# Moving the caps of the activations from GpSimd to VectorE in the feed-forward pipeline of a convolution and attention block

## The reference, cut to what matters

```python
def _quantize_activations_groupwise(x):
    n = x.shape[0]
    gs = n // NUM_GROUPS
    xq = jnp.zeros_like(x)
    for g in range(NUM_GROUPS):
        ag = x[g * gs:(g + 1) * gs]
        gamma = jnp.max(jnp.abs(ag))
        xq = xq.at[g * gs:(g + 1) * gs].set(jnp.clip(ag * QB / (gamma + EPS), -QB + EPS, QB - EPS))
    return xq

def _bitlinear(x, W, b):
    Wb = _binarize_weights_groupwise(W)
    y = jnp.einsum('btc,oc->bto', x, Wb) + b
    return _quantize_activations_groupwise(y)

h = _bitlinear(x, W1, b1)                 # 96 -> 384 channels
h = jax.nn.gelu(h, approximate=False)
out = _bitlinear(h, W2, b2)               # 384 -> 96 channels
```

## Time and profile before

| | us |
|---|---|
| median of three runs | 3130.85 (3129.27 to 3132.96) |
| the profiled execution | 3126.59 |
| its span in the trace | 3124.9 |
| TensorE busy | 2841.3 (91%) |
| VectorE busy | 2173.1 (70%) |
| ScalarE busy | 2052.4 (66%) |
| GpSimd busy | 1393.8 (45%) |

### The profile page before, as it was taken

One profiled execution on the slowest core, in us unless ns is written; L12 is line 12 of the kernel. 1 busy time (PEld: TensorE's weight loads), 2 busy tenths in 40 slices (PEclk: granted clock), 3 DMA queues, 4 the chain that ended last, 5 costly groups with the idle time before them and its releaser, 6 DMA issues. The chain is left out here.

```text
span 3124.9 us, 85427 instructions
## 1 busy us (share of the span) xinstructions
PE 2841.3 (91%) x28774; PEld 1733.4 (55%) x28966; DVE 2173.1 (70%) x4403; ACT 2052.4 (66%) x3943; POOL 1393.8 (45%) x2063
## 2 busy tenths in 40 slices
PE   3899999999998589999999999999999979999883
PEld 2445455454544256666666666666666645555541
DVE  3565665656566378888898898889888935455542
ACT  2677777777776357777777777777777745666561
POOL 0143444444343444434444444443444413577778
PEclk9999999999999789999999999999999989999996
DMA  1113232322222367655556565565655523234434
GB/s 32 41 51 107 71 106 70 106 80 96 97 93 82 112 125 117 120 111 119 115 115 119 112 119 116 115 120 111 119 115 115 117 67 96 81 98 125 126 98 107
DMA packets 919803, 315.97 MB, mean 101 GB/s; under 512 B 848257, under 2 KB 904354, under 8 KB 919714
## 3 DMA queue, kind: packets, MB, share of 16 engines
q1 hardware_dynamic: 916258, 313.98, 42.4%
q10 hardware_dynamic: 3456, 0.79, 0.1%
HBM read 113.35 MB, written 99.88 MB: 68 GB/s over the span
## 5 line engine op out<-in xcount | busy, mean ns | idle before, releaser
L939 DVE TENSOR_REDUCE at_unit_max<-at_ps_queries 128x1 f32<-128x512 f32 (+3 forms) x2304 | 1121.1, 548 | 119.7 <-PE at_ps_queries L831 97.5
L905 ACT ACTIVATE at_probs<-at_ps_keys 128x512 f32<-128x512 f32 x1344 | 738.5, 596 | 244.7 <-PE at_ps_keys L845 216.7
L831 PE MATMUL at_ps_queries<-at_turned 96*128 96x512 bf16 (+3 forms) x2304 | 688.0, 330 | 64.3 <-DMA at_turned<-at_spread 31.8
L845 PE MATMUL at_ps_keys<-at_turned 128*128 128x128 bf16 (+3 forms) x3264 | 593.8, 268 | 2.9 <-ACT at_probs L905 2.4
L845 PEld LDWEIGHTS at_ps_keys<-at_turned 128*128 128x128 bf16 x3456 | 255.4, 97 | 241.1 <-ACT at_probs L905 122.6
L865 PE MATMUL at_ps_values<-at_probs,at_v 128*32 128x128 f32 x10752 | 373.4, 276 | 0.5 <-ACT at_probs L905 0.5
L799 POOL TENSOR_TENSOR at_tick<-at_one 128x1 f32<-128x1 f32 x192 | 37.1, 193 | 705.5 <-ACT at_diag_probs L905 460.2
L834 PE MATMUL at_ps_queries<-mask_queries,ident_bf 128*128 128x128 bf16 x1536 | 338.8, 221 | 0.0
L865 PEld LDWEIGHTS at_ps_values<-at_probs,at_v 128*32 128x32 f32 x10752 | 270.6, 109 | 42.3 <-ACT at_probs L905 1.3
L1189 POOL TENSOR_SCALAR ff_hidden<-ff_hidden 128x1024 f32<-128x1024 f32 x90 | 246.9, 2769 | 63.6 <-ACT ff_hidden L1147 63.6
L831 PEld LDWEIGHTS at_ps_queries<-at_turned 96*128 96x128 bf16 x2304 | 217.5, 98 | 100.7 <-DMA at_turned<-at_spread 32.9
(11 more groups left out here) (199 smaller groups left out, 4896.4 us busy)
## 6 DMA issues: line engine op xcount, KB each, us to landing
qkv_rows<-cb_packed SPq DMA_DIRECT2D x32, 1536.0 KB, 8.3
at_stacks<-qkv_rows SPq DMA_DIRECT2D x192, 256.0 KB, 3.2
cb_x<-in_x_dram SPq DMA_DIRECT2D x32, 384.0 KB, 3.7
cb_x_again<-in_x_dram SPq DMA_DIRECT2D x32, 384.0 KB, 4.5
x_after_conv<-cb_x SPq DMA_DIRECT2D x32, 384.0 KB, 5.0
attention_rows<-at_att SPq DMA_DIRECT2D x384, 32.0 KB, 2.1
ff_att_rows<-attention_rows SPq DMA_DIRECT2D x32, 384.0 KB, 3.7
ff_x<-x_after_conv SPq DMA_DIRECT2D x32, 384.0 KB, 4.7
```

What stands on the lines that cost most here:

```text
L831: mm = pe.matmul(pq[:, u % QBANKS, 0:n], QT[0:STACK, slot, qb * P:(qb + 1) * P], KT[0:STACK, slot, k0:k0 + n], start=True, stop=True)
L845: mm = pe.matmul(pk[:, bank_k, c0:c0 + n * P], KT[:, slot, kb * P:(kb + 1) * P], QT[:, slot, q0 * P:(q0 + n) * P], start=(c0 == 0), stop=True,
L905: act.activation(probs, pk[:, (slot * NU + k) % KBANKS, :], ACT.Exp, scale=scale).then_inc(S["probs"], 1)
L939: dve.tensor_reduce(MX[:, r % 2, qb, k0 // BANK:k0 // BANK + 1], pq[:, u % QBANKS, 0:n], AX.X, ALU.max).then_inc(S["unit_max"], 1)
```

## The change

The caps of the activations (`limit`) move from GpSimd's program to VectorE's. For a group's first image caps 0 and 1 stand behind X2 and cap 2 behind the last maximum of the round; for the other images all three stand near the start of the round, ahead of the maximum over Y2. In VectorE's round the first maximum, `peak1(r, 0)`, moves ahead of the wait for GpSimd's power, and the second, `peak1(r, 1)`, moves from before X2 to behind it. GpSimd keeps the power and the output cap (`cap`), and computes that of the next output o + 1 after the power; that of a group's first output stands ahead of the power. In the last group VectorE computes the output caps of images 24 to 27 itself (with a semaphore of their own, `limited_late`), GpSimd those of 28 and 29. SyncE's, TensorE's and ScalarE's programs are unchanged.

```diff
--- before.py
+++ after.py
@@ -1002,7 +1002,7 @@
         b2_loaded = sem("b2_loaded")
         names = ("ones_set half_set att_turned att_copied y_done x2_ready xc_done squares var_sums scale xn_ready "
                  "xn_turned xnt_ready y1_psum y1_copied y1_max max1 all_max1 scale1 gelu h_ready y2_psum y2_ready "
-                 "y2_max max2 all_max2 scale2 limited out_ready").split()
+                 "y2_max max2 all_max2 scale2 limited limited_late out_ready").split()
         S = {n: sem(n) for n in names}
 
         def quarters(dram):
@@ -1184,29 +1184,26 @@
 
             @block.gpsimd
             def _(pool):
-                def limit(s, k):
-                    pool.wait_ge(S["gelu"], 3 * s + k + 1)
-                    pool.tensor_scalar(Y1[:, s % SLOTS, k, :], Y1[:, s % SLOTS, k, :], LIMIT, None, ALU.min
-                                       ).then_inc(S["h_ready"], 1)
+                def cap(o):
+                    pool.wait_ge(S["scale2"], 2 * (o // GB) + 2)
+                    pool.tensor_scalar(Y2[:, o % SLOTS, :, :], Y2[:, o % SLOTS, :, :], M2[:, o // GB, 3:4], LIMIT,
+                                       ALU.mult, ALU.min).then_inc(S["limited"], 1)
+
                 pool.memset(MINUS_HALF[:, :], -0.5).then_inc(S["half_set"], 1)
                 pool.memset(SQ[:, :, C:C + 1], 1e-5).then_inc(S["half_set"], 1)
                 pool.wait_ge(S["half_set"], 2)
                 for r in range(-1, FULL + OUT_LAG):
-                    m, s, o = r + 1, r - LAG, r - OUT_LAG
+                    m, o = r + 1, r - OUT_LAG
+                    if 0 <= o < FULL - GB and o % GB == 0:
+                        cap(o)
                     if 0 <= m < FULL:
                         pool.wait_ge(S["var_sums"], m + 1)
                         _above(pool.wait_ge, S["xn_ready"], m)
                         pool.tensor_tensor(SCALE[:, :], VS[:, :], MINUS_HALF[:, :], ALU.pow).then_inc(S["scale"], 1)
-                    if o >= 0:
-                        pool.wait_ge(S["scale2"], 2 * (o // GB) + 2)
-                        pool.tensor_scalar(Y2[:, o % SLOTS, :, :], Y2[:, o % SLOTS, :, :], M2[:, o // GB, 3:4], LIMIT,
-                                           ALU.mult, ALU.min).then_inc(S["limited"], 1)
-                    if 0 <= s < FULL and s % GB == 0:
-                        for k in range(CHUNKS):
-                            limit(s, k)
-                    if 0 <= s + 1 < FULL and (s + 1) % GB:
-                        for k in range(CHUNKS):
-                            limit(s + 1, k)
+                    if 0 <= o + 1 < FULL - GB and (o + 1) % GB:
+                        cap(o + 1)
+                for o in (FULL - 2, FULL - 1):
+                    cap(o)
 
             @block.vector
             def _(dve):
@@ -1229,6 +1226,11 @@
                                       ).then_inc(S[scale_name], 1)
                     dve.wait_ge(S[scale_name], 2 * g + 1)
                     dve.reciprocal(M[:, g, 3:4], M[:, g, 2:3]).then_inc(S[scale_name], 1)
+
+                def limit(s, k):
+                    dve.wait_ge(S["gelu"], 3 * s + k + 1)
+                    dve.tensor_scalar(Y1[:, s % SLOTS, k, :], Y1[:, s % SLOTS, k, :], LIMIT, None, ALU.min
+                                      ).then_inc(S["h_ready"], 1)
 
                 def peak1(n, k):
                     dve.wait_ge(S["y1_copied"], 6 * n + 2 * k + 2)
@@ -1243,6 +1245,9 @@
                         group_scale(M1, r // GB - 1, "all_max1", "scale1")
                     if o >= 0 and o % GB == 0:
                         group_scale(M2, o // GB, "all_max2", "scale2")
+                    if 0 <= s < FULL and s % GB:
+                        for k in range(CHUNKS):
+                            limit(s, k)
                     if 0 <= s - 1 < FULL:
                         dve.wait_ge(S["y2_ready"], s)
                         dve.tensor_reduce(G2[:, (s - 1) // GB % 2, (s - 1) % GB:(s - 1) % GB + 1],
@@ -1254,6 +1259,8 @@
                         dve.wait_ge(S["squares"], m + 1)
                         _above(dve.wait_ge, S["scale"], m)
                         dve.tensor_reduce(VS[:, :], SQ[:, :, :], AX.X, ALU.add).then_inc(S["var_sums"], 1)
+                        if 0 <= r < FULL:
+                            peak1(r, 0)
                         dve.wait_ge(S["scale"], m + 1)
                         _above(dve.wait_ge, S["xn_turned"], m)
                         for a in range(2):
@@ -1261,9 +1268,8 @@
                                                     xc[:, a, :].rearrange("p (t c) -> p t c", c=C),
                                                     _bcast(SCALE[:, 4 * a:4 * a + 4], 2, C), ALU.mult)
                         ins.then_inc(S["xn_ready"], 1)
-                    if 0 <= r < FULL:
+                    elif 0 <= r < FULL:
                         peak1(r, 0)
-                        peak1(r, 1)
                     if n < BATCH:
                         dve.wait_ge(S["y_done"], n + 1)
                         dve.wait_ge(x_loaded[n % 2], 16 * (n // 2 + 1))
@@ -1272,14 +1278,26 @@
                         dve.scalar_tensor_tensor(out=X2[:, n % 3, :], in0=py[0:C, :], scalar=w["bp"][:, 0:1],
                                                  in1=X1[:, n % 2, :], op0=ALU.add, op1=ALU.add
                                                  ).then_inc(S["x2_ready"], 1)
+                    if 0 <= s < FULL and s % GB == 0:
+                        limit(s, 0)
+                        limit(s, 1)
                     if 0 <= r < FULL:
+                        peak1(r, 1)
                         peak1(r, 2)
                         if r % GB == GB - 1:
                             column_of_maxima(M1, r // GB, G1, "y1_max", 3 * (r + 1), "max1")
+                    if 0 <= s < FULL and s % GB == 0:
+                        limit(s, 2)
                     if r >= 2 * GB and r % GB == 0 and r < FULL + LAG + 1:
                         max_of_row(M2, r // GB - 2, "max2", "all_max2")
                     if o >= 0:
-                        dve.wait_ge(S["limited"], o + 1)
+                        if FULL - GB <= o < FULL - 2:
+                            dve.wait_ge(S["scale2"], 2 * (o // GB) + 2)
+                            dve.tensor_scalar(Y2[:, o % SLOTS, :, :], Y2[:, o % SLOTS, :, :], M2[:, o // GB, 3:4], LIMIT,
+                                              ALU.mult, ALU.min).then_inc(S["limited_late"], 1)
+                            dve.wait_ge(S["limited_late"], o + 1 - (FULL - GB))
+                        else:
+                            dve.wait_ge(S["limited"], o + 1 if o < FULL - GB else o + 1 - (GB - 2))
                         dve.wait_ge(xr_loaded[o % 4], 64 * (o // 4 + 1))
                         _above(dve.wait_ge, stored[o % 4], 64 * (o // 4))
                         dve.scalar_tensor_tensor(out=OUT[:, o % 4, :, :], in0=Y2[:, o % SLOTS, :, :], scalar=-LIMIT,
```

## The result

The changed kernel takes **3060.3 us** (median of 4 runs, 3058.5 to 3063.0) beside 3130.1 us before in the same session (4 runs, 3127.5 to 3133.0): ratio 0.9774, interval 0.9761 to 0.9787. Forecast were 3062 us and a range of 3049 to 3081. The profiled execution took 3058.6 us, span 3056.9, mean clock 0.975; the span before was 3124.9.

A forecast was written before the change was run, and what follows sets the result against it. Ordinary rounds were taken as bound by TensorE plus a late X2, the tail by GpSimd. Savings of 36.4 - 0.2 + 33.0, taken as 69 us, from 3126.6 gave 3057.6; the median's 4.3 us offset made 3062, range 3049 to 3081.

The forecast's parts named there:

- Prices: Moved instructions on VectorE: 0.70 us for each of 90 activation caps, 0.62 us for each of four late output caps.
- Contention: Where a VectorE cap meets a GpSimd cap, the VectorE instruction was charged 0.85 us.
- Ordinary rounds: Rounds without a group's start: TensorE's wait for X2 goes, nothing on VectorE is late; 14.5 us, from 15.41.
- Last into first: Three intervals from a group's last round into the next group's first: 15.1 us, from 15.98.
- First rounds: Four intervals of a group's first round, with GpSimd's run of six caps before: 16.65 us, from 18.96.
- Tail: Last blocks: 5.35 us cycles, block 24 slowed by half clock, then SyncE's queue late next; 33.0 us saved.
- Total: Whole kernel: 36.4 - 0.2 + 33.0 = 69.2 us saved, taken as 69; median 3062 us.
- Dear caps (1): Rival: a VectorE activation cap costs 1.21 us, lengthening groups' first rounds and the last blocks; 3071 us, 12%.
- Full block (2): Rival: each meeting of VectorE and GpSimd costs a GpSimd instruction's length, 12 us in the last blocks; 3076 us, 12%.
- The clock (3): Rival: TensorE, idling in the last blocks, partly falls to half clock again, costing 10 us; 3072 us, 10%.
- Late X2 (4): Rival: L1107, not the maxima, releases X2, so 19 rounds stay 0.9 us longer, 17 us; 3079 us, 6%.
- VectorE as the bound (5): Rival: VectorE bounds every round once caps exceed 1.7 us, its room being 5.1 us; 3160 us at 2.77, 3%.

The follow-up runs named there:

- e6: Changed kernel with the stores of the last group's six images issued from ScalarE's queue, loads left to SyncE; 3053.3 us, ratio 0.9756.
- e5: Changed kernel with all six output caps of the last group on GpSimd again, none on VectorE; 3060.1 us, ratio 0.9775.
- e4: Changed kernel with two more caps of the same size, into a tile nothing reads, ahead of each activation cap on VectorE; 3103.9 us, ratio 0.9905.
- e7: Changed kernel without the 90 activation caps, so TensorE waits for the activation itself; 3051.1 us, ratio 0.9742.
- e8: Changed kernel with three more caps of the same size, into a tile nothing reads, ahead of each activation cap on VectorE; 3143.0 us, ratio 1.0041.
- e1: Kernel before with VectorE's new order of the maxima alone, all caps staying on GpSimd; 3103.3 us, ratio 0.9907.
- e2: Changed kernel with VectorE's old order of the maxima, both ahead of X2, caps staying on VectorE; 3074.6 us, ratio 0.9820.
- e9: Changed kernel with all six last-group output caps on GpSimd and the last group's stores issued by ScalarE; 3061.1 us, ratio 0.9770.

## Why the prediction was right

**Prices.** The cap was taken at 0.70 us; 0.69 is the median recorded, 0.60 what it occupies in a row. The late output cap: 0.62 predicted, 0.61 to 0.62 where it is alone. **Contention** was charged at 0.85 us; a VectorE cap that met a GpSimd cap took 1.26 to 1.31 us, 0.6 more. The charge on GpSimd's side was missing: six output caps in the tail took 22.61 us and not the 17 of the prediction. One output waited 0.57 us for them (3006.80), off the path, so it cost nothing.

**Ordinary rounds.** 14.5 predicted, 14.57 measured, with the stall gone and nothing late in its place. **Last into first**: 15.1 and 15.14. **First rounds**: 16.65 (its own terms, 9.35, 0.3 and 6.95, add to 16.60) and 16.07 (16.38 in the first group). Over-sized was cap 2: it was put behind both maxima and ends at + 7.3, not + 7.85, because caps and maxima overlap at their edges. The sum of the 23 intervals: 343.9 predicted, 342.7 measured.

Two of the rounds counted as ordinary had lost 1.7 us each to the clock before, which the prediction does not mention. That did no harm, since its sum is made from what a round takes after the change.

**Tail.** Cycle 5.35 predicted, 5.45 measured; block 24's multiplication, partly at half clock, 6.8 and 6.92; 33.0 us and 33.0. SyncE's queue was named as what is late next, and the last two outputs wait for its loads; e6 took 4 us off there.

**Total.** 69.2 predicted, 68.0 by the two spans with the stage begun 3.8 us later, 69.8 by the two medians of the session. Between the same anchors it is 71.8 (37.6, 33.0 and the 1.2 of rounds -2 to 5, which were forecast to lose 0.2 and can't be read so closely). The start of the stage moves by up to 7 us from one execution to another, and the forecast median was set 4.3 us above the profiled time where it came 1.7 above: the terms were right, and that the medians meet within 2 us is in part luck.

**Rivals.** Dear caps (1): no, 0.69 us. Full block (2): no as a mechanism; a VectorE instruction that met a GpSimd cap was 0.6 to 0.9 us longer and never 2.85, and GpSimd's cap 0.8 us longer beside one output sum (e5), more beside several VectorE instructions (the longest cap took 4.17 us in the changed kernel and 4.66 in e4). The Trainium skill's page "SBUF — State Buffer" (section "SBUF: two separate sides") has a lock held for the whole instruction, and what VectorE lost here does not agree with it. The clock (3): half speed in 2995 to 3000, as priced for block 24, and full from 3005 on; e7 shows what that stretch costs, 2.8 us. Late X2 (4): no; X2 starts 0.04 us after L1107's end, and L1122 does not wait. VectorE as the bound (5): e8 shows it in the ordinary rounds, with a room of 5.7 us and not 5.1.

**What the reasoning had wrong** did not show in the total. It counted the long rounds behind a group's first as ordinary ones, which it took to lose 0.84 us to the late X2 where they lost 2.0 to 3.7, so the expectation of e1 was 11 us too high (3114 and 3103.3). In the sum this did no harm, since with both halves those rounds become ordinary by either reading. A prediction of the order alone, made with the same steps, would have been as far off.

## What to carry to other kernels

Look at what an engine's program order puts ahead of the instruction that the bound engine waits for: here, taking two maxima from in front of X2, one into the wait for the power and one behind it, was worth 24 us by the trace and 28 by medians with no engine relieved, and 14 once the caps had moved (e2 against the changed kernel). When a simple operation is moved to a faster engine, count its whole row of such instructions against the idle time in that engine's round; the round breaks at that room and not at the engine's busy share, and the rounds with the least slack, a group's first, break well before the others. When two parts of a change shorten the same rounds, each alone looks worth more than it adds.

## What the runs showed that was not expected

One meeting of the two engines can come out either way. In e5, VectorE's output (0.96 us) ran at its full speed and GpSimd's cap was the longer, 3.63 us a cap; in e9 the same pair, the output starting within 0.1 us of a cap's end in both kernels, left GpSimd at 2.83 and stretched VectorE's output to 1.65. What decides it was not tried, and in these two traces it was worth 4 us at the end of the kernel; the medians (0.9775 and 0.9770) don't show that, and e9's profiled execution was its fastest, so how often each comes is open. When both cap at once, as at 2740.84 in the changed kernel, both are longer, by 0.6 and 0.9 us.

A short wait of TensorE can cost more than itself. Behind the same idle time of 1.96 us the multiplication with W2 took 5.78 us in two rounds of the kernel before and 4.09 in another. Nothing here tells which it will be, so the price of a wait near 2 us, taken from one round, can be 1.7 us too low.

A recorded duration is not an occupancy: caps on VectorE are recorded at 0.68 us and follow each other by 0.60, twelve in 7.22 us. Twelve times 0.68 would be 8.2 us.
